# A decoder layer with two attentions and a routed feed-forward part: value products, routing chain and mask transposes placed anew in the second phase

## The chip, the cores and the metric

The kernel runs on one core of a Trainium2 chip. A core has a matrix engine (TensorE, PE in the rows), whose stationary operands are loaded in a queue of their own (PEld), a vector engine (VectorE, DVE), a scalar engine (ScalarE, ACT), a general engine (GpSimd, POOL) and SyncE (SP), which here issues nearly all DMAs. Each engine runs its own instructions in order, and they wait for one another by semaphores. SBUF is the on-chip memory (`mem`), PSUM (`ps`, eight banks) the memory that TensorE writes. The metric is the time of one execution on the device, in microseconds; lower is better.

## The reference

A pre-norm decoder layer on 32 sequences of 100 tokens, 512 wide: unmasked self-attention with 16 heads of 128, a masked cross-attention with 16 heads of 32 over a latent of 128, and a feed-forward part (1408 wide) with eight low-rank experts, of which the two with the largest router probabilities count per token.

```python
x = x + _L0_attn_ref(_layernorm(x), ...)        # q, k normalised, softmax, 16 heads
x = x + _L0_xattn_ref(_layernorm(x), ctx_512, ...)
x = x + _L0_ffn_ref(_layernorm(x), ...)

# _L0_xattn_ref
qp = q @ Wq.T
k, v = jnp.split(latent_kv @ Wkv_expand.T, 2, axis=-1)
scores = jnp.where(causal, einsum('bhqd,bhkd->bhqk', qh, kh) * inv_sqrt_d, min)
out = einsum('bhqk,bhkd->bhqd', softmax(scores), vh) @ Wout.T

# _L0_ffn_ref
probs = softmax(xf @ Wr.T); topw, topi = top_k(probs, 2)
expert_w = sum(one_hot(topi, 8) * topw[..., None], axis=1)
for e in experts:
    h = silu(gate_base + xf @ Ag_e.T @ Bg_e.T * 2) * (up_base + xf @ Au_e.T @ Bu_e.T * 2)
    acc += h @ Ad_e.T @ Bd_e.T * 2 * expert_w[:, e]
out = silu(gate_base) * up_base @ Wd.T + acc
```

## The kernel before

The first phase (to about 1240 us) does the self-attention of all sequences and stays as it is. The second phase does the rest in groups: six of five sequences (500 tokens, four tiles of 125 rows) and one of two (200 tokens, two tiles of 100). Groups 1 to 4 run in a hardware loop (`over_groups`: group 0 ahead of it, then `Fori(1, FULL - 1)`, then groups 5 and 6 behind it), whose body is `layer(g)`, the feed-forward part of group g, followed by `cross_attention(g + 1)`. The order of each engine is written by hand, one program per engine. A product in high precision is three f16 products (`three`, lines 1474 to 1476): high by high, high by low, low by high. So each value that goes into one is split: ScalarE writes the high part, VectorE the low part.

`cross_attention(g)` on TensorE: `turn_row` (1563) transposes the normalised rows, `keys` (1577), `cross_values` (1585: one f32 product for each sequence, into banks 2 and 3 in turn, so that each waits for ScalarE's eviction of the last but one, `take_cv`, 870), `queries` (four times twelve products, evicted by `take_qp`, 875, to banks 0, 1, 4, 5). Then for each sequence b the mask and the scores of 16 heads (1730, 1736) into banks 0 to 3, which wait for the exponentials of b - 1 (ScalarE, 948), the transposes of the probabilities of b - 1 (1748) and the product with the values (`mix`, 1710). Beside them TensorE does the down projection of the group before, in 48 pieces of three products (`project_out`, 1647 to 1649): `OUT_AT` and `OUT_AFTER` say how many stand where. The output projection (`project`) of the first three tiles (`early`) comes during the last sequence, that of the fourth tile behind it. Each tile is then normalised (VectorE 1172), transposed (1563) and split (ScalarE 864, VectorE `row_lo`, 1177).

Then the routing: 48 products of 8 columns (24 in the last group) give the logits in bank 6, and 24 products of 500 columns the experts' factors in banks 4 and 5. VectorE's chain (1379 to 1396), on four tiles of eight logits at once, scales, subtracts the maximum, waits for ScalarE's exponential (978), normalises and picks the first and the second largest. Each operation waits for the one before (`link`). Four copies (1399) spread the two selections, and these times their weights, over 128 rows; TensorE transposes each (1790, "masks" 0 to 3) into banks 2 and 3 in turn, and ScalarE evicts them (982). VectorE multiplies the factors from PSUM by masks 0 and 1 (1408), ScalarE and VectorE split these (986 and 1414, `am_hi` and `am_lo`). Masks 2 and 3 are used after the eleven chunks only (1261).

`layer(g)` on TensorE, for each of eleven chunks j: gate and up products (12 each), the first adapter products (`lora`), which for j = 0 wait for all four `am_lo`, and the down factors of chunk j - 1. When the group's rows are added up, GpSimd copies them from `yn` to `y` (758, `moved`). It first waits for the DMA that stores the last group's output from `y`, and that is issued behind the last output addition (VectorE 1253), just ahead of the logits.

In group 0 three pieces of weights are split beside the attention (`beside_first`), ScalarE's half (795) behind the exponentials of sequence b, VectorE's half (1052) behind its reciprocals.

## Time and profile before

| | us |
|---|---|
| median of 3 runs | 2606.91 |
| lowest, highest | 2603.4, 2607.54 |
| the profiled execution | 2602.67 |
| its span, first to last instruction | 2600.9 |

The rows below come from that one execution. Its mean granted TensorE clock is 0.98 of full. Over the span TensorE is busy 2476.5 us (95%), VectorE 1544.2, ScalarE 1343.1, GpSimd 867.8. A row of the timeline has the start (us from the span's start), the duration, the engine, the line, the operation with its tiles, a count where equal rows are merged, and in brackets how long the engine stood idle before it and who ended that. Ends of TensorE's products are modelled, so they overlap a little. A row of windows has the stretch, its length, the busy time of each engine with its instructions, the mean granted clock (PEclk; 0.50 is 1.2 GHz, 1.00 is 2.4 GHz) and the DMA share.

### The profile page before, as it was taken

What the parts mean: (1) busy time and instruction counts of PE and PEld (TensorE: products, weight loads), DVE (VectorE), ACT (ScalarE), POOL (GpSimd) and SP (SyncE); (2) the same over time, 40 slices, a digit from 0 to 9 for tenths busy, and PEclk for the clock granted to TensorE, in tenths of its full rate; (3) what the DMA queues carried; (4) which work ended last, traced back from release to release, by engine and by line L of the source; (5) the groups of instructions that cost most, each with busy time, mean ns of one, the idle gap of its engine ahead of it and who ended that gap; (6) DMA issues with size and microseconds to landing.
All of it is one profiled execution on the core that took longest, in us unless ns stands there. A gap on an engine that the chain in (4) does not pass through costs nothing.

```text
span 2600.9 us, 47418 instructions
## 1 busy us (share of the span) xinstructions
PE 2476.5 (95%) x16390; PEld 1334.4 (51%) x16390; DVE 1544.2 (59%) x3589; ACT 1343.1 (52%) x4098; POOL 867.8 (33%) x801
## 2 busy tenths in 40 slices
PE   6999999999999999999879999999999999999998
PEld 3555455555554555445454464464464464465466
DVE  7787756666666666667356545555554645645634
ACT  4555555555555555555446544454454554554433
POOL 2343333333333333333123324323323323422413
PEclk9999999999999999999869999999999999999999
DMA  5687777876787678787411001001001001000000
GB/s 155 151 183 169 154 154 158 175 166 148 156 173 156 154 157 185 167 193 162 125 35 34 32 3 35 16 2 37 17 2 37 12 6 37 4 14 24 7 17 8
DMA packets 455394, 235.29 MB, mean 90 GB/s; under 512 B 389096, under 2 KB 391784, under 8 KB 455144
## 3 DMA queue, kind: packets, MB, share of 16 engines
q1 hardware_dynamic: 455144, 232.08, 38.3%
q8 instruction: 142, 2.33, 0.4%
q14 instruction: 108, 0.88, 0.1%
HBM read 78.66 MB, written 32.77 MB: 43 GB/s over the span
## 4 chain that ended last, share of the span: by engine, by line
PE 84%; DVE 7%; ACT 4%; issue 3%; POOL 1%; DMA 1%; SPq 1%; DVEq 0%; POOLq 0%; ACTq 0%
PE ps L1474 22%; PE ps L1475 22%; PE ps L1476 22%; PE ps L1647 3%; PE ps L1648 2%; PE ps L1649 2%; ACT mem L948 2%; PE ps L1748 2%; PE ps L1657 1%; PE ps L1661 1%; PE ps L1659 1%; PE ps L1585 1%; PE ps L1736 1%; PE ps L1710 1%; PE ps L1730 1%
## 5 line engine op out<-in xcount | busy, mean ns | idle before, releaser
L1474 PE MATMUL ps<-mem 128*128 128x512 f16 (+6 forms) x3924 | 1203.5, 326 | 50.4 <-issue 23.3
L1475 PE MATMUL ps<-mem 128*128 128x512 f16 (+6 forms) x3924 | 1216.6, 325 | 0.0
L1476 PE MATMUL ps<-mem 128*128 128x512 f16 (+6 forms) x3924 | 1199.9, 325 | 0.0
L1474 PEld LDWEIGHTS ps<-mem 128*128 128x128 f16 (+3 forms) x3924 | 407.0, 104 | 370.8 <-issue 66.1
L1476 PEld LDWEIGHTS ps<-mem 128*128 128x128 f16 (+3 forms) x3924 | 408.4, 104 | 311.5 <-issue 9.2
L1475 PEld LDWEIGHTS ps<-mem 128*128 128x128 f16 (+3 forms) x3924 | 409.8, 104 | 300.4 <-issue 9.6
L736 POOL TENSOR_TENSOR mem<-mem 128x500 f32<-128x500 f32 (+1 forms) x231 | 268.6, 1163 | 358.3 <-ACT mem L1016 174.4
L686 POOL TENSOR_TENSOR mem<-mem 128x8 f32<-128x8 f32 x100 | 163.7, 1637 | 517.3 <-DVE mem L1090 517.3
L830 ACT ACTIVATE mem<-ps,mem 100x100 f32<-100x100 f32 x512 | 169.2, 345 | 223.2 <-DVE mem L1120 222.1
L1428 DVE TENSOR_TENSOR mem<-mem 128x500 f16<-128x500 f32 (+1 forms) x231 | 144.4, 648 | 179.7 <-ACT mem L998 175.3
L698 POOL TENSOR_TENSOR mem<-mem 100x400 f16<-100x400 f32 x128 | 158.8, 1241 | 173.1 <-ACT mem L840 173.1
L750 POOL TENSOR_TENSOR mem<-mem 100x400 f32<-100x400 f32 x128 | 108.1, 852 | 306.8 <-DVE mem L1309 306.8
L810 ACT ACTIVATE mem<-ps 128x512 f32<-128x512 f32 x200 | 117.8, 589 | 171.2 <-DVE mem L1084 90.9
L998 ACT ACTIVATE mem<-mem 128x500 f16<-128x500 f32 (+1 forms) x231 | 127.9, 585 | 112.1 <-POOL mem L736 111.7
L1151 DVE SCALAR_TENSOR_TENSOR mem<-ps,mem 128x512 f32<-128x512 f32 x100 | 68.9, 689 | 182.1 <-PE ps L1476 182.0
L948 ACT ACTIVATE mem<-ps,mem 100x100 f32<-100x100 f32 x512 | 168.3, 375 | 12.4 <-DVE mem L1293 12.2
L820 ACT ACTIVATE mem<-ps,mem 128x128 f16<-128x128 f32 x400 | 114.0, 368 | 83.6 <-POOL mem L686 83.6
L1084 DVE TENSOR_REDUCE mem<-mem 128x4 f32<-128x512 f32 x200 | 135.9, 679 | 32.1 <-ACT mem L810 32.0
L1439 DVE TENSOR_TENSOR mem<-ps,mem 128x500 f32<-128x500 f32 (+1 forms) x154 | 97.2, 631 | 71.0 <-PE ps L1476 70.7
L1098 DVE SCALAR_TENSOR_TENSOR mem<-ps,mem 128x128 f32<-128x128 f32 x400 | 112.0, 342 | 38.1 <-POOL mem L686 38.1
L692 POOL TENSOR_TENSOR mem<-mem 100x400 f32<-100x400 f32 x128 | 109.1, 852 | 72.3 <-DVE mem L1130 72.3
L1647 PE MATMUL ps<-mem 128*125 128x512 f16 (+1 forms) x312 | 122.2, 392 | 3.2 <-DVE mem L1268 1.9
(123 smaller groups left out, 3134.4 us busy)
## 6 DMA issues: line engine op xcount, KB each, us to landing
x<-mem SPq DMA_DIRECT2D x100, 256.0 KB, 2.9
mem<-x SPq DMA_DIRECT2D x75, 256.0 KB, 3.4
mem<-in_x SPq DMA_DIRECT2D x50, 256.0 KB, 3.6
mem<-x SPq DMA_DIRECT2D x12, 1000.0 KB
mem<-mem SPq DMA_DIRECT2D x32, 200.0 KB
out<-mem SPq DMA_DIRECT2D x6, 1000.0 KB
mem<-in_wq SPq DMA_DIRECT2D x16, 256.0 KB, 4.0
mem<-in_wk SPq DMA_DIRECT2D x16, 256.0 KB, 4.4
```

The lines of the kernel that those rows point to most:

```text
L686: pool.tensor_tensor(rr[:, u % 2, :], ms[:, u % 2, :], half[:, 0:2 * HG], ALU.pow).then_inc(s["rr"], 1)
L698: pool.tensor_tensor(p_split[0:S, n % 2, 1, :, 0:S], probs[0:S, :, :], p_split[0:S, n % 2, 0, :, 0:S], ALU.subtract).then_inc(s["plo"], 1)
L736: pool.tensor_tensor(hh[:, i, 0:gs], gate[:, i, 0:gs], ub[:, 0:gs] if i == 0 else up[:, i - 1, 0:gs], ALU.mult).then_inc(c["h"], 1)
L830: op = act.activation(probs[0:S, h, :], ps_s[0:S, h * S:(h + 1) * S], ACT.Exp, bias=mx[0:S, h:h + 1], accum_out=den[0:S, h:h + 1])
L948: op = act.activation(cprobs[0:S, i, m, :], ps[0:S, i, m * S:(m + 1) * S], ACT.Exp, bias=cmx[0:S, i, m:m + 1], accum_out=cden[0:S, i, m:m ...
L998: act.activation(hb_hi[:, jj, 0:gs] if i == 0 else hs_hi[:, i - 1, 0:gs], hh[:, i, 0:gs], ACT.Copy).then_inc(c["hhi"], 1)
L1084: dve.tensor_reduce(ss[:, i, m * HG:(m + 1) * HG], sq[:, :, :], AX.X, ALU.add).then_inc(s["ss"], 1)
L1428: dve.tensor_tensor(lo, hh[:, i, 0:gs], hi, ALU.subtract).then_inc(c["hlo"], 1)
L1474: pe.matmul(out_ap, ah, bh, start=(i == 0), stop=False)
L1475: pe.matmul(out_ap, ah, bl, start=False, stop=False)
L1476: mm = pe.matmul(out_ap, al, bh, start=False, stop=(i == len(pairs) - 1))
L1647: pe.matmul(ps[0:tm, 7, :], h_hi, w_hi, start=(j == 0), stop=False)
```

## The change

Values, in groups 1 to 6: two ahead of the queries (banks 2, 3), the third behind them (bank 6, once the down factors' sum has been read), the fourth and fifth behind the scores of the first sequence (banks 5, 4), these two evicted by VectorE. Routing: the chain works on the logits as they are in PSUM. It subtracts the maximum, finds the first largest, lowers it by 1e30, finds the second; the exponentials (now two on ScalarE) are taken beside it, and only the weights need them. Copies 0 and 1 come ahead of the weights. Masks 0 and 1 are transposed ahead of the gate products of chunk 0, masks 2 and 3 behind them; the products with masks 0 and 1 no longer wait for masks 2 and 3. In group 0 the logits and factors of the first three tiles are computed before the fourth tile is transposed. VectorE's half of the three weight pieces goes behind the next sequence's maxima. `OUT_AFTER` is (8, 4) instead of (6, 6).

```diff
-        OUT_AT, OUT_AFTER = {}, (6, 6)
+        OUT_AT, OUT_AFTER = {}, (8, 4)
...
+        V_BANKS, V_ACT = (2, 3, 6, 5, 4), 3
+        def values_taken(g):
+            return g * V_ACT + GB - V_ACT
...
-                    for b in range(nb):
-                        take_cv(g * GB, b)
+                    for b in range(2):
+                        take_cv(g * GB, b, V_BANKS[b])
...
+                    for b in range(2, min(nb, V_ACT)):
+                        take_cv(g * GB, b, V_BANKS[b])
...
-                act.wait_ge(c["top"], g + 1)
-                act.activation(rt["p"][0:tm, 0:nt, :], rt["p"][0:tm, 0:nt, :],
-                               ACT.Exp).then_inc(c["rexp"], 1)
-                for k in range(4):
+                act.wait_ge(c["chain"], g * LINKS + 2)
+                act.activation(rt["p"][0:tm, 0:nt, :], rt["l"][0:tm, 0:nt, :], ACT.Exp,
+                               scale=1 / (X_SCALE * W_SCALE)).then_inc(c["rexp"], 1)
+                act.wait_ge(c["chain"], g * LINKS + 7)
+                act.activation(col["w2"][0:tm, 0:nt], col["m2"][0:tm, 0:nt], ACT.Exp,
+                               scale=1 / (X_SCALE * W_SCALE)).then_inc(c["rexp"], 1)
+                def take_mask(k):
                     act.wait_ge(c["mT"], g * 4 + k + 1)
                     act.activation(msk[:, k, 0:gs], ps[:, 2 + k % 2, 0:gs],
                                    ACT.Copy).then_inc(c["mTe"], 1)
+                take_mask(0)
+                take_mask(1)
                 for i in range(4):
                     act.wait_ge(c["am"], g * 4 + i + 1)
                     act.activation(am_hi[:, i, 0:gs], tmp[:, i, 0:gs], ACT.Copy).then_inc(c["ahi"], 1)
+                    if i % 2:
+                        take_mask(2 + i // 2)
...
+                def take_values(b):
+                    dve.wait_ge(c["v"], g * GB + b + 1)
+                    dve.tensor_scalar(cv[0:S, b, :], ps[0:S, V_BANKS[b], :], CV_SCALE, None,
+                                      ALU.mult).then_inc(c["ved"], 1)
...
+                        for k in (range(V_ACT, nb) if last_nb and b == 0 else []):
+                            take_values(k)
+                        for n in (beside_first(b - 1) if b and not last_nb else []):
+                            split_b_lo(n)
                         for i in range(4):
                             invert_sum(b, i)
-                        for n in (beside_first(b) if not last_nb else []):
-                            split_b_lo(n)
...
-                for t in early:
-                    if t < 2:
-                        row_lo(g * 2 * NT + nt, t, tm, t)
+                first = len(early) if not last_nb else min(2, len(early))
+                for t in range(first):
+                    row_lo(g * 2 * NT + nt, t, tm, t)
                 for t in range(len(early), nt):
                     norm(t)
-                for t in range(min(2, len(early)), nt):
+                for t in range(first, nt):
...
-                lg, p, a, z = (rt[n][0:tm, 0:nt, :] for n in "lpab")
-                link(dve.tensor_scalar(lg, ps[0:tm, 6, 0:nt * NE].rearrange("p (t e) -> p t e", e=NE),
-                                       1 / (X_SCALE * W_SCALE), None, ALU.mult))
-                link(dve.tensor_reduce(col["m"][0:tm, 0:nt], lg, AX.X, ALU.max))
-                dve.tensor_tensor(p, lg, wide("m"), ALU.subtract).then_inc(c["top"], 1)
-                dve.wait_ge(c["rexp"], g + 1)
-                link(dve.tensor_reduce(col["d"][0:tm, 0:nt], p, AX.X, ALU.add))
-                link(dve.reciprocal(col["r"][0:tm, 0:nt], col["d"][0:tm, 0:nt]))
-                link(dve.tensor_tensor(p, p, wide("r"), ALU.mult))
-                for k, w in enumerate(("w1", "w2")):
-                    link(dve.tensor_reduce(col[w][0:tm, 0:nt], p, AX.X, ALU.max))
-                    link(dve.tensor_tensor(a, p, wide(w), ALU.is_equal))
-                    link(dve.tensor_tensor(a, a, rank[0:tm, 0:nt, :], ALU.mult))
-                    link(dve.tensor_reduce(col["m"][0:tm, 0:nt], a, AX.X, ALU.max))
-                    link(dve.tensor_tensor(sel[k][0:tm, 0:nt, :], a, wide("m"), ALU.is_equal))
-                    link(dve.tensor_tensor(sel[2 + k][0:tm, 0:nt, :], sel[k][0:tm, 0:nt, :], wide(w),
-                                           ALU.mult))
-                    if k == 0:
-                        link(dve.scalar_tensor_tensor(out=p, in0=sel[0][0:tm, 0:nt, :], scalar=-2.0,
-                                                      in1=p, op0=ALU.mult, op1=ALU.add))
-                for k in range(4):
+                lg, p, a, rest = (rt[n][0:tm, 0:nt, :] for n in "lpab")
+                rl = ps[0:tm, 6, 0:nt * NE].rearrange("p (t e) -> p t e", e=NE)
+                def spread_out(k):
                     dve.tensor_copy(spread[0:tm, 0:nt, k, :, :],
                                     sel[k][0:tm, 0:nt, :].unsqueeze(3).to_broadcast([tm, nt, NE, R])
                                     ).then_inc(c["spread"], 1)
 
+                def first_of(k, values):
+                    link(dve.scalar_tensor_tensor(out=a, in0=values, scalar=0.0,
+                                                  in1=rank[0:tm, 0:nt, :], op0=ALU.is_equal,
+                                                  op1=ALU.mult))
+                    link(dve.tensor_reduce(col["m"][0:tm, 0:nt], a, AX.X, ALU.max))
+                    link(dve.tensor_tensor(sel[k][0:tm, 0:nt, :], a, wide("m"), ALU.is_equal))
+                link(dve.tensor_reduce(col["m"][0:tm, 0:nt], rl, AX.X, ALU.max))
+                link(dve.tensor_tensor(lg, rl, wide("m"), ALU.subtract))
+                first_of(0, lg)
+                link(dve.scalar_tensor_tensor(out=rest, in0=sel[0][0:tm, 0:nt, :], scalar=-1e30,
+                                              in1=lg, op0=ALU.mult, op1=ALU.add))
+                link(dve.tensor_reduce(col["m2"][0:tm, 0:nt], rest, AX.X, ALU.max))
+                link(dve.tensor_tensor(rest, rest, wide("m2"), ALU.subtract))
+                first_of(1, rest)
+                spread_out(0)
+                spread_out(1)
+                dve.wait_ge(c["rexp"], g * 2 + 2)
+                link(dve.tensor_reduce(col["d"][0:tm, 0:nt], p, AX.X, ALU.add))
+                link(dve.reciprocal(col["r"][0:tm, 0:nt], col["d"][0:tm, 0:nt]))
+                link(dve.tensor_tensor(col["w2"][0:tm, 0:nt], col["w2"][0:tm, 0:nt],
+                                       col["r"][0:tm, 0:nt], ALU.mult))
+                for k, w in enumerate(("r", "w2")):
+                    link(dve.tensor_tensor(sel[2 + k][0:tm, 0:nt, :], sel[k][0:tm, 0:nt, :], wide(w),
+                                           ALU.mult))
+                spread_out(2)
+                spread_out(3)
 
                 for i in range(4):
                     if i == 0:
-                        dve.wait_ge(c["mTe"], g * 4 + 4)
+                        dve.wait_ge(c["mTe"], g * 4 + 2)
...
-                    for b in range(nb):
-                        cross_values(g, b)
+                    pe.wait_ge(c["cke"], g * KC + 2)
+                    for b in range(2):
+                        cross_values(b, V_BANKS[b])
                     pe.wait_ge(c["lnlo"], g * 2 * NT + nt)
                     for m in range(KC):
                         queries(g, gs, m)
-                pe.wait_ge(c["ve"], g * GB + nb)
+                    pe.wait_ge(c["dsum"], g)
+                    for b in range(2, min(nb, V_ACT)):
+                        cross_values(b, V_BANKS[b])
+                else:
+                    pe.wait_ge(c["ve"], GB)
...
+                            elif last_nb and i >= 2:
+                                pe.wait_ge(c["ve"], values_taken(g - 1) + V_ACT + i - 1)
...
+                        for k in (range(V_ACT, nb) if last_nb and b == 0 else []):
+                            cross_values(k, V_BANKS[k])
...
+                def route(a, b):
+                    mm = None
+                    pe.wait_ge(c["lnlo"], g * 2 * NT + nt + b)
+                    for t in range(a, b):
+                        mm = three(ps[0:tm, 6, t * NE:(t + 1) * NE], [
+                            (yT_hi[:, e, t * tm:(t + 1) * tm], yT_lo[:, e, t * tm:(t + 1) * tm],
+                             wr_hi[:, e, :], wr_lo[:, e, :]) for e in range(KC)])
+                    return mm
+                def factors(a, b):
+                    for bank, hi, lo in ((4, ag_hi, ag_lo), (5, au_hi, au_lo)):
+                        mm = three(ps[:, bank, a:b], [
+                            (hi[:, e, :], lo[:, e, :], yT_hi[:, e, a:b], yT_lo[:, e, a:b])
+                            for e in range(KC)])
+                        if b == gs:
+                            mm.then_inc(c["a"], 1)
+                if last_nb:
+                    for t in range(min(2, len(early)), nt):
+                        turn_late(t)
+                    some_out(OUT_AFTER[1])
+                    route(0, nt).then_inc(c["rl"], 1)
+                    factors(0, gs)
+                else:
+                    for t in early[2:]:
+                        turn_late(t)
+                    route(0, len(early))
+                    factors(0, len(early) * tm)
+                    for t in range(len(early), nt):
+                        turn_late(t)
+                    route(len(early), nt).then_inc(c["rl"], 1)
+                    factors(len(early) * tm, gs)
...
-                for k in range(4):
+                def turn_mask(k):
...
+                turn_mask(0)
+                turn_mask(1)
...
+                    else:
+                        turn_mask(2)
+                        turn_mask(3)
...
+                        pe.wait_ge(c["mTe"], g * 4 + 4)
```

What stands in a row on TensorE at the start of group 1's attention, before: five values (1585) between the transposes and the queries (1474 to 1476).

```order
L1563 MATMUL ps<-mem 128x125 [waits c_yn,c_lnlo]
L1563 MATMUL ps<-mem 128x125 x3
L1585 MATMUL ps<-mem 100x512 [waits c_cke] x2
L1585 MATMUL ps<-mem 100x512 [waits c_ve] x3
L1474 MATMUL ps<-mem 128x500 [waits c_lnlo]
L1475 MATMUL ps<-mem 128x500
L1476 MATMUL ps<-mem 128x500
```

And of the change, from the end of the queries on: a value (1616), mask and scores (1774, 1780), two values, the first piece of output (1682). Three of the five values have moved, and the waits for ScalarE's evictions of values (`c_ve`) with them.

```order
L1511 MATMUL ps<-mem 128x500
L1616 MATMUL ps<-mem 100x512 [waits c_dsum]
L1774 MATMUL ps<-mem 100x400 [waits c_qpe,c_cke]
L1774 MATMUL ps<-mem 100x400
L1774 MATMUL ps<-mem 100x400 [waits c_ve] x2
L1780 MATMUL ps<-mem 100x100 x16
L1616 MATMUL ps<-mem 100x512 x2
L1682 MATMUL ps<-mem 125x512 [waits c_dlo]
```

VectorE in the loop's body, the end of the routing chain before: the copies (1399) stand behind all links, and the products with the masks (1408) wait for a mask count (1407) of four.

```order
L1392 TENSOR_TENSOR mem<-mem 125x32 [waits c_chain]
L1372 REGISTER_ALU
L1393 TENSOR_TENSOR mem<-mem 125x32 [waits c_chain]
L1372 REGISTER_ALU
L1399 COPY mem<-mem 125x4x128 [waits c_chain]
L1399 COPY mem<-mem 125x4x128 x3
L1406 ISA
L1407 ISA [waits c_mTe]
L1408 SCALAR_TENSOR_TENSOR mem<-ps,mem 128x500 [waits c_a]
```

The same place of the change: two copies (1405) come behind the second selection (1415), ahead of the weights (1428 on).

```order
L1414 TENSOR_REDUCE mem<-mem 125x4 [waits c_chain]
L1395 REGISTER_ALU
L1415 TENSOR_TENSOR mem<-mem 125x32 [waits c_chain]
L1395 REGISTER_ALU
L1405 COPY mem<-mem 125x4x128 [waits c_chain]
L1405 COPY mem<-mem 125x4x128
L1427 ISA
L1428 TENSOR_REDUCE mem<-mem 125x4 [waits c_rexp]
```

TensorE in group 0, before: the transposes of tiles 2 and 3 (1563), each behind its norm, and then all the logits (columns of 8).

```order
L1476 MATMUL ps<-mem 125x512
L1563 MATMUL ps<-mem 128x125 [waits c_yn]
L1563 MATMUL ps<-mem 128x125 x3
L1563 MATMUL ps<-mem 128x125 [waits c_yn]
L1563 MATMUL ps<-mem 128x125 x3
L1474 MATMUL ps<-mem 125x8 [waits c_lnlo]
```

And of the change: tile 3's transposes (1598) stand behind the factors of the first three tiles (375 columns), and its own twelve logit products behind them.

```order
L1509 MATMUL ps<-mem 128x375
L1510 MATMUL ps<-mem 128x375
L1511 MATMUL ps<-mem 128x375
L1598 MATMUL ps<-mem 128x125 [waits c_yn]
L1598 MATMUL ps<-mem 128x125 x3
L1509 MATMUL ps<-mem 125x8 [waits c_lnlo]
```

## Rows read from the trace of the kernel before

**Rows 1.** Windows: group 0 up to its feed-forward part; one full group.

```profile
1240.00:1376.00 136.00, 109.73 (x811) 66.47 (x810) 64.95 (x145) 61.16 (x233) 27.02 (x38) 0.76 0.24 71
...
1689.60:1888.80 199.20, 194.23 (x1261) 104.60 (x1262) 106.33 (x221) 99.04 (x293) 65.17 (x59) 0.99 0.05 18
```

**Rows 2.** Waits of TensorE, second phase: total us, times, longest us.

```profile
PE ps L1730 <- ACT mem L948: 11.0, 14, 2.1
...
PE ps L1790 <- DVE mem L1399: 7.2, 4, 2.6
...
PE ps L1730 <- ACT mem L875: 4.4, 6, 0.8
```

**Rows 3.** Timeline, TensorE, group 1, values to second scores.

```profile
1474.51 4.60 PE L1585 MATMUL ps<-mem 128*100 128x512 f32 x10
...
1490.06 0.85 PE L1730 MATMUL ps<-mem 100*100 100x400 bf16 x4 [0.77 <-ACT mem L875]
...
1496.51 0.37 PE L1730 MATMUL ps<-mem 100*100 100x400 bf16 x1 [0.33 <-ACT mem L948]
...
1497.81 0.37 PE L1730 MATMUL ps<-mem 100*100 100x400 bf16 x1 [0.93 <-ACT mem L948]
```

**Rows 4.** Timeline, VectorE, group 1: last two row splits.

```profile
1475.05 1.25 DVE L1177 TENSOR_TENSOR mem<-ps,mem 128x500 f16<-128x500 f32 x2
```

**Rows 5.** Windows of TensorE behind the waits of group 1.

```profile
1498.00:1504.00 6.00, 6.00 (x58) 0.72 0.01 3
```

**Rows 6.** Timeline, group 3: VectorE's chain, TensorE's first mask.

```profile
1958.40 0.19 DVE L1379 TENSOR_SCALAR mem<-ps 125x32 f32<-125x32 f32 x1 [2.34 <-PE ps L1476]
...
1964.36 0.19 DVE L1390 TENSOR_TENSOR mem<-mem 125x32 f32<-125x32 f32 x1 [2.35 <-issue]
...
1965.75 1.07 PE L1790 MATMUL ps<-mem 125*128 125x125 f32 x8 [2.58 <-DVE mem L1399]
```

**Rows 7.** Timeline, groups 1, 3, 5: GpSimd's copy and what follows it.

```profile
1569.48 3.60 POOL L758 TENSOR_TENSOR mem<-mem 125x2048 f32<-125x2048 f32 x1 [17.33 <-DMA out<-mem]
...
1570.86 2.43 DVE L1408 SCALAR_TENSOR_TENSOR mem<-ps,mem 128x500 f32<-128x500 f32 x4 [3.70 <-ACT mem L982]
...
1575.70 0.39 PE L1474 MATMUL ps<-mem 128*128 128x500 f16 x1 [0.51 <-DVE mem L1414]
...
1967.12 3.60 POOL L758 TENSOR_TENSOR mem<-mem 125x2048 f32<-125x2048 f32 x1 [17.93 <-DMA out<-mem]
...
1972.18 2.44 DVE L1414 TENSOR_TENSOR mem<-mem 128x500 f16<-128x500 f32 x4
...
2365.28 3.60 POOL L758 TENSOR_TENSOR mem<-mem 125x2048 f32<-125x2048 f32 x1 [17.12 <-DMA out<-mem]
...
2367.62 3.56 DVE L1414 TENSOR_TENSOR mem<-mem 128x500 f16<-128x500 f32 x4
...
2371.24 0.39 PE L1474 MATMUL ps<-mem 128*128 128x500 f16 x1 [1.53 <-DVE mem L1414]
```

**Rows 8.** Timeline, GpSimd, group 6.

```profile
2532.89 1.89 POOL L758 TENSOR_TENSOR mem<-mem 100x1024 f32<-100x1024 f32 x1 [16.11 <-DMA out<-mem]
```

**Rows 9.** Timeline, ScalarE, group 0: first exponential of two steps.

```profile
1306.22 0.34 ACT L948 ACTIVATE mem<-ps,mem 100x100 f32<-100x100 f32 x1 [0.32 <-DVE mem L1293]
...
1316.02 0.34 ACT L948 ACTIVATE mem<-ps,mem 100x100 f32<-100x100 f32 x1 [0.47 <-DVE mem L1293]
```

**Rows 10.** Timeline, group 0, VectorE and TensorE, around the last norm.

```profile
1348.29 1.25 DVE L1177 TENSOR_TENSOR mem<-ps,mem 128x500 f16<-128x500 f32 x2
...
1349.46 3.38 DVE L1172 TENSOR_SCALAR mem<-mem 125x512 f32<-125x512 f32 x1
...
1352.90 1.10 PE L1563 MATMUL ps<-mem 125*128 125x125 f32 x4 [5.97 <-DVE mem L1172]
...
1368.49 1.02 PE L1790 MATMUL ps<-mem 125*128 125x125 f32 x8
```

**Rows 11.** Window of TensorE, group 0: its 48 logit products.

```profile
1355.39:1360.53 5.14, 5.14 (x48) 0.50 0.38 148
```

44 lines of the change are left out of this document (20 added, 24 removed).

## The prediction

> **What bounds the kernel now.** I read the stretches first. The second phase, from about 1240 us on, is the only part that the change touches. In the stretch of one full group TensorE is busy 194.23 of 199.20 us at a mean clock of 0.99; in the stretch in front of the first group's feed-forward part it is busy 109.73 of 136.00 us at 0.76 [rows 1]. So TensorE is the bound, its work stays as it is, and what can be won is its idle time and its time at the lower clock. The list of waits names the idle time: over all seven groups 11.0 and 4.4 us before the scores of the second attention (for the exponentials, and for the queries' evictions) and 7.2 us before the masks' transposes [rows 2]. Everything below asks which of these the change reaches and what is late next there.
>
> I number the groups 0 to 6; 1 to 5 are alike, with one before them and a short one (two sequences) behind.
>
> **Values (groups 1 to 5).** Before, five value products run in a row, 4.60 us, and 0.77 us is lost before the first scores, to the last query's eviction [rows 3]. After the first scores and six down-projection pieces TensorE waits 0.33 and then 0.93 us for the exponentials, since ScalarE needs longer for 16 of them than TensorE has work [rows 3]. The stretch from the first value to the second scores' end is 24.5 us. The change puts two values ahead of the queries, one behind them (beside that eviction) and two between the first scores and the pieces. No work goes away: five values stay 5 x 0.86 us (the 4.60 us less the drain of the last, and 0.17 us of bank hand-off that goes, as each value has its own bank). The third value covers the 0.77 us except about 0.05; the last two, 1.7 us, cover the 1.26 us. What is late next: the queries now wait for the last row split, which ends at 1475.05 + 1.25 = 1476.30 us where two values end at 1474.51 + 1.72 = 1476.23 [rows 3, 4], so 0.1 us comes back. VectorE's two new evictions stand before its reciprocals, about 1.2 us, but those feed transposes that come 5 us later, so they cost nothing; without that cover they would cost 1.2 us a group. Sum: 0.77 + 1.26 + 0.17 - 0.05 - 0.1 = 2.05, say 2.0 us, five times 10.0 us. In group 1 the clock fell to 1.2 GHz right behind this wait: over 1498 to 1504 us its mean is 0.72 [rows 5], and 6 x 0.28 = 1.7 us of dense work was lost. With no wait ahead I let that go: 1.7 us. Group 6 has two values and gains nothing.
>
> **Chain and masks (groups 0 to 6).** Before, 19 small VectorE operations (0.19 us, one every 0.226 us) and a trip to ScalarE stand ahead of the first copy for a mask: from 1958.40 us on, with one stall of 2.35 us in VectorE's own issue that three iterations of the loop show at the same instruction [rows 6]. TensorE then waits 2.58 us in group 3 [rows 6]. After, the first copy comes behind eleven operations, 2.5 us, and the stall, if it stays about 30 instructions behind the jump, falls behind the first two copies. TensorE's factor products take 5.1 us, so that wait goes entirely. The masks 2 and 3 come behind the gate products, so their 0.34 us of hand-off goes too, and the splits of the scaled factors need only masks 0 and 1.
>
> But the next thing in line is not this chain. GpSimd copies the 125x2048 rows of y, 3.60 us, once the output store of the last group has landed [rows 7]; that hangs on the last output addition and not on the routing. In group 5 VectorE's four splits (am_lo) took 3.56 us instead of 2.44 in group 3: they were due at 2367.62 and the copy ended at 2368.88. The products that come before them, which read PSUM, ran through the copy in group 1 at their normal 2.43 us [rows 7]. So the split waits for the copy's end and the first adapter product comes 2.36 us behind it, as in group 5 (2371.24). By my chain the splits would be ready 9.3 to 9.8 us after the logits; the copy runs from 8.4 to 12.7 (in group 3 it starts 8.7 us behind the chain's first operation [rows 6, 7]). They collide in every one of the groups 1 to 5. The adapter product then stands at copy end + 2.36: in group 1 at 1573.08 + 2.36 = 1575.44 against 1575.70, in group 3 at 1970.72 + 2.36 = 1973.08 against 1974.79 (there it was right behind the splits, 1972.18 + 2.44), in group 5 nothing [rows 7]. Groups 2 and 4, worked out alike, give 0.77 and 0.68. Sum 0.26 + 0.77 + 1.71 + 0.68 + 0 = 3.4 us. The waits that go come back as one wait of 1 to 3 us before the adapter product. Bounds: -1 us if GpSimd's first product slips ahead of the last split or a clock drop follows the wait of group 3; 12.3 us if nothing collides (the product then 6.8 us of TensorE work behind the first mask, saving 1.2, 2.0, 4.4, 2.3 and 2.4 us). I take 3.4, as [rows 7] shows both the block and its cause.
>
> The Trainium skill, "GPSIMD Engine Reference", Specifications, says that GpSimd shares its SBUF interface with VectorE and that there is contention with VectorE instructions in a 2-port mode or with two SBUF inputs. By this rule am_lo (two SBUF inputs) is held and the product from PSUM is not, and the trace agrees (3.56 against 2.44, and 2.43 us). It speaks against the gain that the shorter chain promises.
>
> Group 6: its wait of 2.6 us is the longest of that line [rows 2], but GpSimd's copy there ends at 2532.89 + 1.89 = 2534.78 us [rows 8], and GpSimd's first product, which the down factors need, is queued behind it. I give 0.
>
> **First group.** Three pieces of weights are split during its attention. VectorE's half ran ahead of the next scores' maxima; ScalarE waited 0.32 and 0.47 us for these in two steps [rows 9]. The change puts it behind the maxima: 0.8 us. Then the two-part routing. Before, TensorE waits 5.97 us for the norm of the last tile, which took 3.38 us instead of 0.54 beside GpSimd's copy, and the first mask comes at 1368.49 [rows 10]. After, the row split of tile 2 goes ahead of that norm and ends near 1350.1 us (three of 0.6 behind 1348.29), so TensorE has 36 logit products and 24 factor products over 375 columns during the copy. The clock is at half by then, TensorE having been idle for 3 us; it was at half all through the 48 logit products before, 5.14 us of them [rows 11]. At 5.14 / 48 = 0.107 us and at 375 / 1200 = 0.31 us each, and 0.16 once the clock returns (I say near 1356.5, behind dense work as in group 1), they end at about 1358.5. Then tile 3's transposes 0.6, its splits 1.4 (TensorE waits), 12 logit products 0.7: logits at 1361.3, beside which 24 factor products over 125 columns, 0.06 each, and then eleven links and one copy, 2.9 us: first mask at 1364.3, 4.2 us earlier. To the adapter product it was 7.95 us from there and is now 7.2. The 24 more products cost 0.2. If the clock comes back as much later as it was down in group 1, 1.7 us less. I take 3.5 us; bounds 1 to 5.
>
> **Pieces of output 8 and 4 instead of 6 and 6.** Between the last projection and the logits only the place of the late transposes moves, by 1.3 us. Neither side waits there, 4 pieces (2.6 us) still cover the 1.7 us of splits: 0.
>
> **Sum.** 10.0 + 1.7 + 3.4 + 0.8 + 3.5 = 19.4 us. The profiled execution took 2602.67 us (span 2600.9), so it would take 2583.3. It lies 4.24 us under the median of 2606.91, which three runs spread over 2603.4 to 2607.54; the same difference from the median gives 2587.5 us.
>
> **Rivals.**
> 1. No collision (the copy does not hold the splits, or lands early enough): 8.9 us more, 28.3 in all, 2578.6 us. For it: nothing but that the order was never tried. Against: [rows 7] and the norm in [rows 10]. Chance 0.12.
> 2. The gains come back at once: the last two values delay the pieces so that nothing was idle to fill, the clock stays low in the first group, and the wait before the adapter product brings the half clock in two or three groups (1.7 us each). Values 6, first group 2, chain 0: 8 to 12 us, 2597 us. For it: in group 3 a wait of 2.58 us was followed by a stretch at half clock. Against: 1.53 us in group 5 was not. Chance 0.2.
> 3. The program does not do what it says: the order shows the value products and the masks where the diff wants them, so this could only be the issue stall sitting before the first copy. Then only the copy's end counts as before: no change of the sum, below 1 us. So it has no time and no chance of its own.
> 4. Slower. The output store lands later, since its wait is the one thing the adapter product now hangs on in five groups: each microsecond of the store costs five. It turns the sum of 19.4 into a loss from 3.9 us per group on; at 5 us it gives 2612. For it: the copy starts 8.4 to 9.1 us behind the logits, a spread of 0.7 us only. Against: nothing on SyncE or in the store's neighbourhood is moved. Chance 0.03.
>
> **How the numbers follow.** The forecast has 0.65, its own range 2582 to 2593 (first group 1 to 5 instead of 3.5, two losses of 1.7 us to the clock either way). With rival 1 below and rival 2 above, 2578 to 2598 leaves out about 2 in 10. A measurement of this kernel tells 0.2%, 5.2 us, from no change. Faster by more: forecast, rival 1 and nearly all of rival 2, 0.95; within: 0.03; slower 0.02.
>
> **What would show it.** Right: no wait of line 1730's scores for the exponentials or for the query eviction in groups 1 to 5, and one of 0.1 us before the queries; no wait before the first mask in groups 1 to 5; a wait of 1 to 3 us before the first adapter product there, ending 2.4 us behind GpSimd's copy; VectorE's splits over 2.44 us long for four; first mask of group 0 at 1364 us instead of 1368.5. Wrong: splits that run through the copy (rival 1); half clock behind these waits in most groups (rival 2); a copy more than 9.1 us behind the logits (rival 4).

## The result and the profile after

The changed kernel takes **2592.49 us** (median of 5 runs, 2589.72 to 2596.59), the kernel before on the same chip 2606.91 us (5 runs, 2601.02 to 2611.19). The ratio is 0.9951, with a 95% interval of 0.994 to 0.9961, so 0.4 to 0.6% faster: 14.4 us between the medians where 19.4 were forecast. The profiled execution after took 2594.01 us (span 2592.2), only 8.7 us less than the profiled one before. The first phase, which the change does not touch, took 1.5 us more in it: TensorE's first wait among the second attention's scores ends at 1289.22 us before and at 1290.70 after. From there to the end of the span it is 1311.7 us before and 1301.5 after, 10.2 us less. Over the traces of all twelve kernels of this document that wait ends anywhere from 1288.0 to 1294.4 us, so a few microseconds between the times of two single executions say little by themselves.

The list of TensorE's waits in the second phase after the change (line that waits, what it waits for, total us, times, longest us). L1509 is the first of the three products that make one exact product, L1449 the subtraction (`am_lo`) that was L1414 before, L1863 the mask's transpose, L1774 the scores:

```profile
PE ps L1509 <- DVE mem L1449: 16.4, 6, 4.0
...
PE ps L1774 <- ACT mem L955: 5.4, 5, 2.1
...
PE ps L1863 <- DVE mem L1405: 2.5, 2, 1.8
...
PE ps L1774 <- ACT mem L880: 0.5, 1, 0.5
```

Against [rows 2], the 7.2 us before masks are 2.5 (groups 0 and 6 alone), the 11.0 us before scores are 5.4, all in group 0, and the 4.4 us for the query's eviction are 0.5. At the top stands a line that had 4.2 us before: the products that wait for the subtraction, 16.4 us (15.65 in groups 1 to 5, the rest in group 6). The change took the waits that it was aimed at, and a new one stands behind them.

Values to second scores in group 1, TensorE, the answer to [rows 3]. No row of the stretch has a wait:

```profile
1473.85 1.88 PE L1616 MATMUL ps<-mem 128*100 128x512 f32 x4
...
1485.88 1.02 PE L1616 MATMUL ps<-mem 128*100 128x512 f32 x2
1486.81 0.85 PE L1774 MATMUL ps<-mem 100*100 100x400 bf16 x4
...
1488.48 1.96 PE L1616 MATMUL ps<-mem 128*100 128x512 f32 x4
...
1494.17 0.84 PE L1774 MATMUL ps<-mem 100*100 100x400 bf16 x4
1494.95 0.96 PE L1780 MATMUL ps<-mem 32*100 32x100 f32 x32
```

GpSimd's copy of y (now L763), VectorE's four subtractions, and the first adapter product with its wait, in groups 1 and 3 (compare [rows 7]):

```profile
1565.69 3.69 POOL L763 TENSOR_TENSOR mem<-mem 125x2048 f32<-125x2048 f32 x1 [18.33 <-DMA out<-mem]
...
1565.26 6.88 DVE L1449 TENSOR_TENSOR mem<-mem 128x500 f16<-128x500 f32 x4
...
1572.19 0.60 PE L1509 MATMUL ps<-mem 128*128 128x500 f16 x1 [4.05 <-DVE mem L1449]
...
1961.63 3.60 POOL L763 TENSOR_TENSOR mem<-mem 125x2048 f32<-125x2048 f32 x1 [18.10 <-DMA out<-mem]
...
1962.39 5.14 DVE L1449 TENSOR_TENSOR mem<-mem 128x500 f16<-128x500 f32 x4
...
1967.58 0.39 PE L1509 MATMUL ps<-mem 128*128 128x500 f16 x1 [3.22 <-DVE mem L1449]
```

Four subtractions take 6.88 and 5.14 us, where they need 2.44, and the product comes 2.81 and 2.35 us behind the copy's end (1569.38 and 1965.23). The other waits of this kind are 3.06, 3.04 and 2.28 us, in groups 2, 4 and 5.

Windows of TensorE after (start and end, length, busy us, instructions, granted clock, then DMA share and GB/s): behind the wait of the second attention in group 1 ([rows 5] answered: 0.72 is now 1.00), right behind the adapter wait in groups 1 to 5, and the stretch of 36 logit products and their factor products in group 0:

```profile
1498.00:1504.00 6.00, 5.99 (x90) 1.00 0.01 1
1572.00:1576.00 4.00, 3.81 (x11) 0.57 0.32 125
1770.00:1774.00 4.00, 4.00 (x12) 0.57 0.33 126
1968.00:1972.00 4.00, 4.00 (x12) 0.57 0.33 126
2166.00:2170.00 4.00, 4.00 (x13) 0.57 0.32 125
2362.00:2366.00 4.00, 4.00 (x19) 1.00 0.19 59
...
1350.80:1361.00 10.20, 10.20 (x58) 0.52 0.27 103
```

Behind the waits of 3.0 to 4.1 us, TensorE runs dense work at 1.2 GHz for a while; behind the one of 2.28 us it does not. The length of the wait alone does not decide it: in the kernel with group 0 routed in one part (below), where these waits are 1.8 to 3.1 us, a half-clock stretch follows the 2.30 us of group 5 and none the 2.61 us of group 4. In the kernel before, groups 1 to 4 had one such window too (1759 to 1763 us: 0.58), but ahead of the adapter product: among the factor products, and in group 3 behind the wait for the first mask.

### The profile page after: what moved, and what is told of

Its sections match the earlier page's. It is cut to its first block, busy times and chain, and to the rows that moved or that the text cites. A ratio compares the mean times of both kernels' runs of the same rounds, so it can differ in the third digit from the quotient of the medians.

```text
span 2592.2 us, 47471 instructions
## 1 busy us (share of the span) xinstructions
PE 2473.8 (95%) x16414; PEld 1335.5 (52%) x16414; DVE 1558.7 (60%) x3578; ACT 1337.1 (52%) x4095; POOL 870.1 (34%) x801
## 3 DMA queue, kind: packets, MB, share of 16 engines
q8 instruction: 139, 2.28, 0.4%
## 4 chain that ended last, share of the span: by engine, by line
PE 84%; DVE 6%; issue 4%; ACT 2%; POOL 1%; DMA 1%; SPq 1%; DVEq 0%; POOLq 0%; ACTq 0%
PE ps L1509 22%; PE ps L1510 22%; PE ps L1511 22%; PE ps L1682 3%; PE ps L1683 2%; PE ps L1684 2%; PE ps L1796 2%; PE ps L1780 1%; PE ps L1692 1%; PE ps L1696 1%; PE ps L1694 1%; PE ps L1616 1%; PE ps L1752 1%; PE ps L1774 1%; ACT mem L955 1%
## 5 line engine op out<-in xcount | busy, mean ns | idle before, releaser
L1509 PE MATMUL ps<-mem 128*128 128x512 f16 (+7 forms) x3932 | 1206.3, 326 | 67.0 <-issue 22.2
L1510 PE MATMUL ps<-mem 128*128 128x512 f16 (+7 forms) x3932 | 1219.6, 325 | 0.0
L1511 PE MATMUL ps<-mem 128*128 128x512 f16 (+7 forms) x3932 | 1202.8, 325 | 0.0
L1509 PEld LDWEIGHTS ps<-mem 128*128 128x128 f16 (+3 forms) x3932 | 407.7, 104 | 390.4 <-issue 65.3
L1036 ACT ACTIVATE mem<-mem 128x500 f32<-128x500 f32 (+1 forms) x154 | 89.1, 578 | 70.1 <-DVE mem L1474 70.1
```

The source lines that it names most:

```text
L1509: pe.matmul(out_ap, ah, bh, start=(i == 0), stop=False)
L1510: pe.matmul(out_ap, ah, bl, start=False, stop=False)
L1511: mm = pe.matmul(out_ap, al, bh, start=False, stop=(i == len(pairs) - 1))
```

## The ledger of the second phase, group by group

Three distances make the account. The first is from the first logit product of one group to that of the next; the second, from that product to the start of GpSimd's copy; the third, to the first adapter product. Each is a difference between the starts of two rows of the timelines of one execution of each kernel. "Late copy" is the experiment below.

| us | before | after | late copy |
|---|---|---|---|
| logits of group 1 to 2 | 197.90 | 198.40 | 192.54 |
| 2 to 3 | 199.14 | 197.77 | 194.21 |
| 3 to 4 | 199.90 | 197.78 | 194.24 |
| 4 to 5 | 199.08 | 197.61 | 194.22 |
| logits to copy, group 1 | 11.35 | 12.34 | 14.52 |
| logits to copy, group 3 | 11.95 | 12.11 | 16.17 |
| logits to adapter product, group 1 | 17.57 | 18.84 | no wait |
| group 2 | 18.85 | 18.17 | no wait |
| group 3 | 19.62 | 18.06 | no wait |
| group 4 | 18.75 | 18.04 | no wait |
| group 5 | 17.09 | 17.08 | no wait |

The four distances from logits to logits are 4.5 us shorter after. The values part alone should have made them 8 us shorter (four times 2.0), and the chain 3.4. The last column says what stood in the way: with the copy out of it the four are 20.8 us shorter than before.

## Experiments

Each ran beside the kernel before on the same chip. The table has all ten; behind it come, for each, its edit, the text on record and what follows.

| kernel | median us | before beside it | ratio, 95% interval |
|---|---|---|---|
| late copy | 2579.59 | 2606.57 | 0.9896, 0.9881 to 0.9911 |
| values alone | 2595.59 | 2606.57 | 0.996, 0.9947 to 0.9974 |
| chain and masks alone | 2602.92 | 2606.57 | 0.9992, 0.9983 to 1.0001 |
| change, group 0 routed in one part | 2595.5 | 2606.57 | 0.996, 0.9946 to 0.9973 |
| before, late copy | 2605.69 | 2606.82 | 0.9996, 0.9986 to 1.0006 |
| change, copy in four | 2586.92 | 2606.82 | 0.9929, 0.9907 to 0.9952 |
| change, copy twice | 2620.36 | 2606.82 | 1.005, 1.0033 to 1.0066 |
| chain and masks alone, late copy | 2592.01 | 2606.82 | 0.9946, 0.993 to 0.9963 |
| late copy, pieces 6 and 6 | 2579.46 | 2605.52 | 0.9904, 0.9887 to 0.992 |
| late copy, group 0 in one part | 2578.92 | 2605.52 | 0.9898, 0.9881 to 0.9914 |

**The late copy.** One line more in the changed kernel, in GpSimd's part:

```diff
                 pool.wait_ge(c["x2"], g * NT + nt)
+                pool.wait_ge(c["alo"], g * 4 + 4)
                 pool.tensor_tensor(y[0:tm, 0:nt, :], yn[0:tm, 0:nt, :],
```

> The changed kernel with one wait more: GpSimd's copy of y (L763) also waits for the last subtraction of a group's activation factors (L1449 of the changed kernel), so that copy and subtractions no longer run side by side. Theory A (the subtractions stand behind the copy, and TensorE's wait of 2.28 to 4.05 us before the first adapter product is the copy's, the low clock behind it the wait's): L1449 takes 2.4 us for four instead of 5.1 to 6.9, the wait falls below 1 us in groups 1 to 5, the four stretches at half clock behind it go (1.7 us each), and the time is 13 to 20 us below the changed kernel's 2592.5, so 2572 to 2580. Rival B (the subtractions are late by ScalarE's rounding or by the masks, and the copy only stands beside them): the wait stays above 2 us and the time within 3 us of 2592.5. Rival C (the copy, now later, holds GpSimd's first product of the gate and the value up, and TensorE waits for that instead): the adapter wait goes, but waits before the first down projections grow by 1 to 3 us a group, time 2582 to 2592.

2579.59 us, 12.9 us below the changed kernel. The late copy's waits from 1390 to 2400 us, all of them (the lines stand one lower, L1450 is the subtraction), and the answer for the subtractions' line, after and with the late copy (duration in ns, least, median, largest):

```profile
PE ps L1599 <- DVE mem L1188: 4.1, 5, 0.8
PE ps L1693 <- DVE mem L1464: 1.0, 1, 1.0
PE ps L1613 <- DVE mem L1478: 0.8, 4, 0.2
```

```profile
L1449 DVE TENSOR_TENSOR mem<-mem x28: 354/667/4072, 1372.2 to 2520.6; 128x500 f16<-128x500 f32 x24, 128x200 f16<-128x200 f32 x4
```

```profile
L1450 DVE TENSOR_TENSOR mem<-mem x28: 356/670/675, 1373.7 to 2505.3; 128x500 f16<-128x500 f32 x24, 128x200 f16<-128x200 f32 x4
```

The longest subtraction falls from 4072 to 675 ns and the adapter waits are gone, so theory A's mechanism holds and B is out. C is out in groups 1 to 5: GpSimd's first product starts right behind the copy, and no wait for down factors follows (the 1.0 us stand in group 0, at 1396.57 us, and there C is right by that much).

```profile
1569.61 3.60 POOL L764 TENSOR_TENSOR mem<-mem 125x2048 f32<-125x2048 f32 x1 [20.51 <-DVE mem L1450]
1573.17 1.25 POOL L741 TENSOR_TENSOR mem<-mem 128x500 f32<-128x500 f32 x1
...
1567.00 2.44 DVE L1450 TENSOR_TENSOR mem<-mem 128x500 f16<-128x500 f32 x4
```

The time lies at the upper edge of A's range, since the four stretches at half clock did not go. They moved: the window right behind the place of the old wait is at full clock, but one just behind the logits of group 2 is not, with no wait near it, and so it is behind those of groups 3, 4 and 5 (0.60, 0.57 and 0.61 over four microseconds each). That the wait had brought them on is therefore not shown.

```profile
1568.00:1574.00 6.00, 6.00 (x30) 1.00 0.00 0
1750.00:1754.00 4.00, 4.00 (x20) 0.57 0.52 158
```

**Values alone,** taken over into the kernel before:

```diff
+                    for b in range(2):
+                        cross_values(b, V_BANKS[b])
...
+                    for b in range(2, min(nb, V_ACT)):
+                        cross_values(b, V_BANKS[b])
...
+                        for k in (range(V_ACT, nb) if last_nb and b == 0 else []):
+                            cross_values(k, V_BANKS[k])
```

> The kernel before with the values part alone (two values before the queries, one behind them, the others behind the first scores; no new routing, no split masks, no two-part routing, the weight split of group 0 where it was). Theory A (the values term of my sum is right: 2.0 us in each of groups 1 to 5, nothing comes back): 2597 us, the three waits before the first scores (0.77, 0.33, 0.93) gone. Rival B (the 2.0 us come back at the next wait, before the first adapter product): 2602 to 2607, with that wait 1 to 2 us longer than before's 0.51 to 1.53.

11.0 us faster, between A's 10 and the 11.7 us of its two terms (10.0 and the clock of group 1). B is out as it was put: the adapter waits did not grow (1.11 us at most). But in the profiled execution the waits for masks grew from 7.2 to 11.4 us in four groups, so a part does come back, at another place, and still the total holds.

**Chain and masks alone,** taken over into the kernel before:

```diff
+                link(dve.tensor_reduce(col["m"][0:tm, 0:nt], rl, AX.X, ALU.max))
+                link(dve.tensor_tensor(lg, rl, wide("m"), ALU.subtract))
+                first_of(0, lg)
...
+                turn_mask(0)
+                turn_mask(1)
...
+                    else:
+                        turn_mask(2)
+                        turn_mask(3)
```

> The kernel before with the routing chain and the masks in two halves alone. Theory A (the gain ends at GpSimd's copy: what the first masks save is waited for before the first adapter product, and the clock falls behind that wait in most groups, which takes 1.7 us back where it does): 2601 to 2606 us, adapter waits of 2.3 to 4 us in groups 1 to 5, no waits for masks. Rival B (the masks are worth what the waits before them were, 11.0 and 7.2 us, and little comes back): 2590 to 2596.

3.6 us faster by the medians, in A's range and at the 3.4 us of my sum, though the interval reaches to no change. All waits for masks in groups 1 to 5 are gone, and the adapter waits have grown to 7.6 us in five groups. In group 2 the product stands 2.35 us behind the copy's end:

```profile
1767.13 3.60 POOL L758 TENSOR_TENSOR mem<-mem 125x2048 f32<-125x2048 f32 x1 [18.09 <-DMA out<-mem]
...
1773.08 0.39 PE L1495 MATMUL ps<-mem 128*128 128x500 f16 x1 [1.58 <-DVE mem L1435]
```

A's waits of 2.3 to 4 us are a miss: they are 0.74 to 2.3 us, because in this kernel TensorE spends its stretch at half clock ahead of the wait (over 1758.0 to 1761.3 us its products stand 0.42 us apart instead of 0.21), and the wait takes that up.

**Chain and masks alone, with the late copy** (the line above added to that kernel):

> The kernel before with the routing chain and the split masks alone (as in the run of these alone, 2602.9 us) and the copy behind the subtractions. Theory A (without the collision the shorter chain is worth 12.3 us, the other end of my bounds): 2594 to 2597 us, the adapter waits of groups 1 to 5 below 1 us. Rival B (the chain is worth no more than the 3.6 us measured, and the 12.9 us of the copy come from elsewhere): 2600 to 2604.

14.8 us faster than before: A's side, 2 us below its range, and 2.5 us more than the 12.3 us that the prediction gave as the bound without a collision. That bound left out one thing which the late copy does as well: in group 0 the last norm is no longer held, and the wait for it is 3.12 us instead of 5.97, 2.85 us less. TensorE's only wait for a subtraction from 1390 to 2400 us is 0.3 us:

```profile
PE ps L1496 <- DVE mem L1436: 0.3, 1, 0.3
```

**The kernel before with the late copy:**

> The kernel before, and only GpSimd's copy of y made to wait for the last subtraction of the activation factors. Theory A (before the change the copy cost little, since the masks were late anyway: 0.51 to 1.53 us of adapter waits and one split of 3.56 us): 2600 to 2605 us, so at most half of the 12.9 us that the same edit gave behind the change. Rival B (the edit is worth the same 13 us with either kernel, so it has nothing to do with what the change moved): 2592 to 2596.

1.1 us, with an interval on both sides of nothing: A, 0.7 us above its range. The same line is worth 12.9 us with the change and about nothing without it. The four distances from logits to logits are the same as before to 0.2 us, so in groups 1 to 4 the copy cost nothing so long as the masks were late; the shorter chain moved the subtractions into it. In group 0 it did cost something: the first adapter product comes 30.08 us behind the rows' transposes instead of 33.18, again by the norm. Together these kernels give the chain's worth by the medians: 3.6 us with the copy in the way, 14.8 less 1.1 = 13.7 us without. By the single traces, from the first wait among the second attention's scores to the end, it is 5.1 us (1311.7 to 1306.6) and 9.5 us (1308.0 to 1298.5). The second is the larger either way; its size is known to some 4 us only.

**The copy in four instructions:**

```diff
-                pool.tensor_tensor(y[0:tm, 0:nt, :], yn[0:tm, 0:nt, :],
-                                   one[0:tm, :].unsqueeze(2).to_broadcast([tm, nt, E]),
-                                   ALU.mult).then_inc(c["moved"], 1)
+                for t in range(nt):
+                    op = pool.tensor_tensor(y[0:tm, t, :], yn[0:tm, t, :],
+                                            one[0:tm, :].to_broadcast([tm, E]), ALU.mult)
+                op.then_inc(c["moved"], 1)
```

> The changed kernel with GpSimd's copy of y as four instructions of 125x512 instead of one of 125x2048, no wait more. Theory A (VectorE's instruction is held until GpSimd's running instruction ends, whatever that is): no subtraction takes longer than about 1.6 us instead of 4.07, the subtractions go between the pieces, the adapter wait is 1 to 2.5 us, 2583 to 2590 us. Rival B (VectorE is held as long as GpSimd has such work at all): one subtraction of about 4 us as before, 2590 to 2595 us.

Copy and subtractions in group 1, and the subtractions' line:

```profile
1563.15 5.41 POOL L764 TENSOR_TENSOR mem<-mem 125x512 f32<-125x512 f32 x4 [18.34 <-DMA out<-mem]
...
1562.71 4.96 DVE L1450 TENSOR_TENSOR mem<-mem 128x500 f16<-128x500 f32 x4
...
1567.72 0.39 PE L1510 MATMUL ps<-mem 128*128 128x500 f16 x1 [2.12 <-DVE mem L1450]
```

```profile
L1450 DVE TENSOR_TENSOR mem<-mem x28: 357/1505/1512, 1370.6 to 2514.4; 128x500 f16<-128x500 f32 x24, 128x200 f16<-128x200 f32 x4
```

No subtraction is longer than 1.51 us, as A has it. Most of them are that long: 0.67 us of its own and 0.84 us of waiting, less than one piece. A piece takes 1.03 to 1.22 us in group 0, where only the norm stands beside the four, and 1.47 us (the median of all) beside the subtractions. So the two engines take turns, instruction by instruction, and hold each other. (That the copy takes 5.41 instead of 3.60 us is only in part this: four pieces of 1.03 us are 4.1 us without it.) The waits shrink to 14.1 us from 16.4 over six places, less than A said: in groups 1 to 5 they are 2.1 to 3.2 us, not 1 to 2.5. The time falls by 5.6 us against the changed kernel, though the interval is wide enough to make it anything from 2 us slower to 10 us faster.

**The copy twice:**

> The changed kernel with GpSimd's copy of y made twice, one behind the other, 3.6 us more in each group. Theory A (in groups 1 to 5 the first adapter product stands 2.35 us behind the copy's end): the adapter waits grow by 3.6 us each and the time by 18 us, to 2608 to 2612; the longest subtraction is 4 us still or two are held. Rival B (a subtraction slips in between the two copies, or the second copy overlaps work that needs no such port): waits grow by less than 2 us, 2593 to 2602.

2620.36 us, 27.9 us slower than the changed kernel, more than A's 18 and above its range. In group 1:

```profile
1566.16 3.70 POOL L764 TENSOR_TENSOR mem<-mem 125x2048 f32<-125x2048 f32 x1 [18.32 <-DMA out<-mem]
1569.94 3.91 POOL L767 TENSOR_TENSOR mem<-mem 125x2048 f32<-125x2048 f32 x1
...
1565.74 10.28 DVE L1452 TENSOR_TENSOR mem<-mem 128x500 f16<-128x500 f32 x4
...
1576.07 0.60 PE L1512 MATMUL ps<-mem 128*128 128x500 f16 x1 [7.45 <-DVE mem L1452]
```

A subtraction does slip in between the copies, as B has it, but the next one is held again, and the product still comes 2.2 us behind the second copy's end (1573.85). The five adapter waits sum to 35.3 instead of 15.7 us: 19.6 of the 27.9. The clock takes more. Windows that begin with each group's adapter product (groups 1 to 5), and one among group 4's factor products:

```profile
1576.07:1583.00 6.93, 6.93 (x25) 0.76 0.32 122
1778.08:1785.00 6.92, 6.92 (x27) 0.80 0.33 125
1979.93:1987.00 7.07, 7.07 (x21) 0.60 0.33 125
2183.10:2190.00 6.90, 6.90 (x24) 0.72 0.33 126
2384.47:2391.00 6.53, 6.53 (x22) 0.70 0.06 19
2163.00:2167.00 4.00, 4.00 (x20) 0.57 0.49 159
```

Length times what is missing to 1 is 1.7, 1.4, 2.8, 1.9, 2.0 and 1.7, together 11.5 us, where the changed kernel lost 4 x 0.43 x 4 = 6.9: 4.6 us more. In group 6 the wait for GpSimd's first product is 4.5 instead of 2.5 us. 19.6 + 4.6 + 2.0 = 26.2 of 27.9. So a microsecond of the copy costs five of time (19.6 us for some 3.9 in each of five groups) and something of the clock besides.

**Group 0 routed in one part again,** first in the changed kernel and then behind the late copy:

```diff
-                    route(0, len(early))
-                    factors(0, len(early) * tm)
-                    for t in range(len(early), nt):
-                        turn_late(t)
-                    route(len(early), nt).then_inc(c["rl"], 1)
-                    factors(len(early) * tm, gs)
+                    for t in range(len(early), nt):
+                        turn_late(t)
+                    route(0, nt).then_inc(c["rl"], 1)
+                    factors(0, gs)
```

> The changed kernel with group 0's routing in one part again, and its rows' remainders in the order of before; the shift of the weight split stays. Theory A (the two-part routing is worth 1 to 5 us, 3.5 by my sum): 2593.5 to 2597.5. Rival B (worth nothing, since group 0's first mask came 1.2 us earlier only, in one profiled execution): within 1 us of 2592.5.

> The changed kernel with the late copy (2579.6 us) and group 0's routing in one part again. Theory A (the copy beside the last norm was most of what the two parts save; with the norm at 0.54 us the wait before the last transposes is 3.1 us instead of 5.97): 0.5 to 2.5 us slower than 2579.6, so 2580 to 2582. Rival B (the two parts are worth as much as without the late copy, 3.0 us and more): 2582.6 to 2585.

By the medians the kernel is 3.0 us slower than the change in the first case, in A's range; the two intervals, each about 3 us to either side, overlap. In the second, it is 0.7 us faster than with two parts, and neither theory had that. TensorE in group 0 with two parts (after), and with one part and the late copy:

```profile
1343.88 0.65 PE L1598 MATMUL ps<-mem 125*128 125x125 f32 x4 [1.46 <-DVE mem L1187]
1350.80 0.27 PE L1509 MATMUL ps<-mem 128*125 128x8 f16 x1 [3.25 <-DVE mem L1192]
1363.33 0.22 PE L1509 MATMUL ps<-mem 128*125 128x8 f16 x1 [1.39 <-DVE mem L1192]
1367.29 1.86 PE L1863 MATMUL ps<-mem 125*128 125x125 f32 x8 [1.76 <-DVE mem L1405]
```

```profile
1352.76 1.09 PE L1599 MATMUL ps<-mem 125*128 125x125 f32 x4 [3.12 <-DVE mem L1188]
1355.25 0.27 PE L1510 MATMUL ps<-mem 128*125 128x8 f16 x1 [1.39 <-DVE mem L1193]
```

With two parts the waits are 3.25, 1.39 and 1.76 us. With one part they were 5.97 and 1.39 as long as the norm stood behind the copy [rows 10]; with the late copy the norm takes 0.54 us and they are 3.12 and 1.39. The traces also give a distance in which the first phase has no part, from the rows' transposes (the row with the wait of 1.46 us) to the first adapter product of group 0, which is the product behind the twelve gate and twelve up products:

| us | two parts | one part |
|---|---|---|
| copy beside the norm | 31.91 (the change), 28.63 (copy in four), 28.67 (copy twice) | 30.60 |
| late copy | 28.68, 28.74 (pieces 6 and 6) | 29.13 |

The change's own profiled execution is the odd one. In the four others with two parts the clock is back at full 6.5 us behind the first logit product, and in it not for 10 us. With the copy twice, where the same one copy runs beside the norm at first (start and end, length, busy us, instructions, granted clock, DMA share and GB/s):

```profile
1354.51:1361.00 6.49, 6.49 (x45) 0.50 0.00 0
1361.00:1364.70 3.70, 3.06 (x21) 1.00 0.69 225
```

By these, two parts are worth 1.9 us with the copy beside the norm (30.60 less 28.7) and 0.4 us behind the late copy. So they were in the main a remedy for the same copy. The medians (3.0 us, and 0.7 us the other way) agree with this within their intervals and do not show it by themselves.

**Pieces 6 and 6 again,** behind the late copy:

```diff
-        OUT_AT, OUT_AFTER = {}, (8, 4)
+        OUT_AT, OUT_AFTER = {}, (6, 6)
```

> The changed kernel with the late copy (2579.6 us) and 6 and 6 output pieces around the late transposes again instead of 8 and 4. Theory A (the move of two pieces is worth nothing, the 0 of my sum): within 2 us of 2579.6, the wait of 0.81 us before the late transposes in each group unchanged. Rival B (the two pieces ahead give the norm time, 1.3 us in each of five groups, or the six behind cover the row splits better): 2584 to 2588 us, or 2574 to 2576 us.

2579.46 against 2579.59 us: A, the term of 0 was right, to what such medians can tell.

The best kernel of the series is the changed one with the late copy, with group 0 in one part (2578.92 us) or two (2579.59 us), which these runs can't tell apart; both are 1.0% below the kernel before.

## Why the prediction was right, and where not

The time fell 5.0 us above the forecast and inside its own range (2582 to 2593), 0.5 us from the end. Most of the mechanism was right. Its steps:

- **Values, 10.0 us:** right in kind, a little small. From the first value to the second scores' end it is 22.06 us instead of 24.56 in group 1, 21.97 instead of 24.55 in group 2 and 21.93 instead of 24.56 in group 4: 2.5 to 2.6 us a group, where I had 2.0. What I undersized is the wait for the exponentials. I took the idle that the rows list, 0.33 + 0.93; but the four scores started over 2.43 us (1495.68 to 1498.11) and start over 0.78 us now (1494.17 to 1494.95), 1.65 us less. Without a wait the products start 0.2 us apart, though a row lasts 0.37 us; the idle is counted from a row's end, so each wait costs that difference too, 0.17 us. No wait of 0.1 us shows before the queries.
- **Clock in group 1, 1.7 us:** right, 0.72 to 1.00 in that window.
- **Chain and masks, 3.4 us:** the rule (adapter product 2.36 us behind the copy's end) held in groups 2 to 5, and in group 2 with chain and masks alone. Per group I had 0.26, 0.77, 1.71, 0.68 and 0; the third distance of the ledger gives -1.27, 0.68, 1.56, 0.71 and 0.01. Group 1 is off since its store landed later: the copy starts 12.34 us behind the logits instead of 11.35, and the subtractions ended 0.45 us later behind it than elsewhere. The later copy comes with the values part (12.21 us with values alone, 11.24 with chain and masks alone). Why is open. It is the mechanism of my fourth rival, by 1 us and in one group.
- **The step that failed is the clock, behind the adapter wait.** I gave it two losses in the range and none in the sum. It came in groups 1 to 4, 1.7 us each (4 x 0.43). The kernel before has a stretch at half clock in these groups too, but it stands ahead of the adapter product, where my distances count its removal as a gain, and where a wait behind it takes part of it up. The sum should have carried it over: 6.8 us. With the late copy, where the wait is gone, four such stretches are there all the same, so it is not shown that the wait brings them on; what does is open. This is the clock part of rival 2, in four groups instead of two or three; its other parts (values 6, chain 0) did not come.
- **Weight split, 0.8 us:** from the first wait among the scores to that before the rows' transposes it is 53.18 us instead of 54.04: 0.86. This pair flatters the term. Over all traces the distance is 53.89 to 54.51 us in the five kernels with the split at its old place and 53.18 to 53.74 us in the seven with the new one, 0.5 us between the means.
- **Two-part routing, 3.5 us:** in the profiled execution of the change the first mask came 23.41 us behind the rows' transposes instead of 25.23, so 1.8 us earlier and not 4.2, and the first adapter product 31.91 us behind them instead of 33.18, 1.3 us. From the logits' end on I was right (mask 3.1 us behind it, 3.0 forecast). In this execution the failing step is the clock: I let it return at about 1356.5, 6.4 us behind the first logit product, and over 1350.8 to 1361.0 it is 0.52, so half clock held for all 36 logit and 24 factor products. In the four other traces with this routing it returned after 6.5 us, as forecast, and the mask came 21.8 to 21.9 us and the adapter product 28.6 to 28.7 us behind the transposes: 3.4 and 4.5 us less than before. So the step held more often than not, and the term was not too large. (One sum in it is half a microsecond short: by its own rates the 60 products end near 1359.0 us and not at 1358.5.) This is the whole of group 0's routing, with the shorter chain; two parts against one are the smaller part of it, as above.
- **Group 6, 0; pieces, 0:** right. In group 6 a wait of 2.54 us for GpSimd's first product took the place of that for the masks, and from the first logits to the end of the span it is 78.91 us instead of 78.64.

Added up over the profiled executions, values 12.8, clock in group 1 1.7, chain 1.7, weights 0.9, routing 1.3, less 6.8 for the clock, are 11.6 us against 10.2 measured; 1.4 us are not placed, 0.55 of them behind the logits of group 5. The medians give 14.4 us; the longer stretch at half clock in group 0, some 3 us, is one reason why this execution shows less. The errors of the two sides partly cancelled, and that the time lies in the range owes something to luck: values too small by 2.8, chain too large by 1.7, clock by 6.8.

Rival 1 (no collision, 2578.6 us) did not happen, and the kernel in which the collision is taken out runs in 2579.6 us, near its price. The number is better than its sum: four stretches at half clock, which it counts as gone from their old places, are still there, and the values term is 2.8 us too small.

The Trainium skill, "GPSIMD Engine Reference", Specifications, gives contention with VectorE for instructions with two SBUF inputs or in a 2-port mode. The trace agrees for the subtraction, which has two SBUF inputs (0.67 us alone, 4.07 beside the copy), and for VectorE's products that read PSUM, which the copy does not slow (four take 2.42 us in group 3, where the copy starts 1.58 us behind the first). The norm, with one SBUF input of rows, is held as well (0.54 us alone, 2.80 in group 0 after the change); whether it is in a 2-port mode no trace shows. That the two sides take turns by whole instructions is what the copy in four shows (1.51 us a subtraction, 1.47 us a piece).

## What to carry to other kernels

When a chain is made shorter, look up what another engine starts at a time of its own (here a copy released by a store), and ask whether the shorter chain now runs into it; in groups 1 to 4 the same copy was free before, and after the change it cost 12.9 us. A long GpSimd instruction on SBUF belongs where VectorE only reads PSUM or waits, and one wait puts it there. And do not book as a gain a stretch at half clock that may only change its place: 6.8 us of this forecast were such. Lastly, look at more than one trace before a term is called right or wrong: two terms here (the weight split and group 0's routing) look otherwise in the first pair of traces than in all of them.
